# First attention stage: exponentials taken by ScalarE at two shifted arguments and added, in place of tangents and squares, and sequences started one by one

## The reference

```python
    def _L0_xattn_ref(q, k, v):
        scaled = jnp.einsum('bsd,bse->bde', q, k) * scale     # scale = 1/sqrt(256)
        attn = jax.nn.softmax(scaled, axis=1)
        out = jnp.einsum('bde,bse->bsd', attn, v)
        return out
    x = x + _L0_xattn_ref(_layernorm(x, axis=-1), ctx_2048, ctx_2048)
```

## Time and profile before

| what | value |
|---|---|
| median of 3 runs | 1996.21 us (1995.42 to 1996.57) |
| the profiled execution's own time | 2003.36 us |
| its span in the trace | 2001.6 us |
| mean granted TensorE clock | 0.904 of full speed |
| busy: PE, DVE, ACT, POOL | 81%, 69%, 41%, 30% of the span |
| the stage's first VectorE instruction | 12.98 us |
| the stage's last VectorE instruction ends | 79.77 us (79.35 + 0.42) |
| first VectorE instruction of the next stage | 80.58 us |

### The profile page before, as it was taken

The page is one execution under the profiler, slowest core; times in us unless marked ns, Lnnn a source line. Parts: engine busy times, 40 slices in busy tenths (PEclk is TensorE's granted clock), DMA queues, the critical chain, the costliest instruction groups (busy, mean ns, idle before and its releaser), DMA issues. The chain is left out here.

```text
span 2001.6 us, 30042 instructions
## 1 busy us (share of the span) xinstructions
PE 1613.5 (81%) x9326; PEld 1135.7 (57%) x9326; DVE 1387.7 (69%) x3901; ACT 823.7 (41%) x2380; POOL 605.3 (30%) x739
## 2 busy tenths in 40 slices
PE   3559998879353788988889699999987999799883
PEld 2424434356122466666666488788774555688872
DVE  6679969678796688888888634676555333468875
ACT  1113444457332466666667433333331222244451
POOL 0020003067401777777777430111122000321000
PEclk7579999969665999999999899999997999899996
DMA  1305620010382900000000150000035222522200
GB/s 63 110 1 158 194 101 1 13 67 1 9 156 75 343 1 1 2 1 1 1 1 2 31 173 1 26 12 12 11 144 149 75 87 74 179 103 101 69 25 11
DMA packets 103590, 129.34 MB, mean 65 GB/s; under 512 B 14160, under 2 KB 89136, under 8 KB 99984
## 3 DMA queue, kind: packets, MB, share of 16 engines
q1 hardware_dynamic: 94448, 112.39, 17.7%
q0 software_dynamic: 8992, 15.08, 3.6%
...
## 5 line engine op out<-in xcount | busy, mean ns | idle before, releaser
L2326 PE MATMUL l2fa_psQ<-l2fa_xT,l2f_home 128*128 128x128 f32 x1024 | 124.9, 283 | 0.7 <-DMA l2f_home<-in_L2f_kvT 0.7
L2326 PEld LDWEIGHTS l2fa_psQ<-l2fa_xT,l2f_home 128*128 128x128 f32 x1024 | 121.8, 199 | 3.1 <-issue 1.6
L580 POOL TENSOR_TENSOR l0f_diag<-g_identb,l0f_mask 128x1024 bf16<-128x1024 bf16 x16 | 32.0, 2025 | 227.7 <-PE l0f_psA L836 208.8
L2817 ACT ACTIVATE l2x_probs<-l2x_psS,l2x_nmax 128x128 f32<-128x128 f32 x256 | 90.7, 371 | 10.2 <-DVE l2x_nmax L2731 10.0
L2601 POOL TENSOR_TENSOR l2x_probs<-l2x_probs,l2x_rtotal 128x512 f32<-128x512 f32 x64 | 66.8, 1043 | 90.2 <-DVE l2x_rtotal L2737 90.2
L3102 POOL TENSOR_TENSOR route_rrms<-route_vrms,g_minus_half 128x1 f32<-128x1 f32 x8 | 5.7, 707 | 270.6 <-DVE route_vrms L3124 270.6
L2612 POOL TENSOR_TENSOR l2x_vsm<-l2x_vraw,l2x_smooth_row 128x512 f32<-128x512 f32 x64 | 84.7, 1345 | 3.7 <-ACT l2x_vraw L2851 3.4
...
L3511 DVE COPY moe_xgT<-moe_psX 128x256 f32<-128x256 f32 x47 | 20.0, 425 | 91.1 <-PE moe_psX L3617 91.1
L2962 PEld LDWEIGHTS l2x_psS<-l2x_kT,l2x_qT 128*128 128x128 f32 x512 | 66.8, 192 | 22.3 <-issue 17.9
L1427 ACT ACTIVATE l2fa_probs<-l2fa_psS,l2fa_bias 128x128 f32<-128x128 f32 x128 | 45.2, 365 | 76.6 <-DVE l2fa_bias L1411 76.6
L1040 ACT ACTIVATE l1a_probs<-l1a_psS,l1a_nmax 128x256 f32<-128x256 f32 x128 | 58.9, 472 | 42.1 <-PE l1a_psT L1068 29.7
...
## 6 DMA issues: line engine op xcount, KB each, us to landing
...
```

The lines of the kernel that those rows point to most:

```text
L2326: last = nc.tensor.matmul(psQ[bank][:, j, :], w[:, c, h * HD:(h + 1) * HD], xT[u][:, c, :], start=(c == 0), stop=(c == KC - 1))
L2817: last = nc.scalar.activation(probs[:, n % 2, j, :], psS[:, j, :], ACT.Exp, bias=nmax[:, n % 2, j:j + 1], scale=1.0, accum_out=total[:, n ...
```

## The change

The stage is rewritten. ScalarE takes `Exp` straight from the scores, twice: once with the bias of the maximum and once with a bias an eighth larger (`SHIFT`), each with its row sums (two halves each, so four instructions per sequence, L385 of the changed kernel). VectorE adds the two results (L344) and the two sums (L343). The factor 1 + exp(1/8) that both then carry cancels in the division. The tangent, the three steps of `roots` and the squares are gone, and so is the copy of the keys: TensorE reads `G.ctx` itself. The bias takes two instructions where it took one.

Statistics, power and normalisation are now made per sequence: `statistics(b)` is three VectorE instructions (L321 to L323), GpSimd has one power of a single column per sequence (L313), `normalise(b)` one VectorE instruction (L327). `scores(b)` waits for its own sequence, and statistics of later sequences stand between the work on earlier ones. `scores(b + 2)` waits for `probs_ready` of b, since both exponentials read `psS`. The loops are written out in full. Four semaphores go and one comes.

```diff
 def stage_l0_xattn(nc, G, A):
     with ExitStack() as ctx:
         T = Pool(nc, ctx, "l0a")
         q = T.sb("q", [P, B, D])
         alloc_norm(T)
-        k = T.sb("k", [P, 2, D])
         v = T.sb("v", [P, 2, KC, P])
-        probs = T.sb("probs", [P, 2, KC, D])
-        t = T.sb("t", [P, 2, KC, D])
-        den = T.sb("den", [P, KC, D])
+        probs, probs2 = T.sb("probs", [P, 2, KC, D]), T.sb("probs2", [P, 2, KC, D])
         nmax = T.sb("nmax", [P, 2, KC])
-        bias = T.sb("bias", [P, 2, KC])
-        total = T.sb("total", [P, 2, KC])
+        bias = T.sb("bias", [P, 2, 2, KC])
+        total = T.sb("total", [P, 2, 2, KC])
         rtotal = T.sb("rtotal", [P, 2, KC])
...
         scale = D ** -0.5
+        SHIFT = 0.125
 
         with nc.Block() as block:
             @block.gpsimd
             def _(pool):
-                rstd_all(nc, G, T)
+                for b in range(B):
+                    pool.wait_ge(T.var_ready, b + 1)
+                    nc.gpsimd.tensor_tensor(T.rstd[:, b:b + 1], T.ve[:, b:b + 1], G.minus_half[:, 0:1], ALU.pow)\
+                        .then_inc(T.rstd_ready, 1)
 
             @block.vector
             def _(dve):
-                T.order = Order(dve, order)
-                normalise_all(nc, G, T, q)
-                def maxima(b, u):
+                o = Order(dve, order)
+
+                def statistics(b):
+                    o.step(nc.vector.bn_stats(T.stats[:, b, :], G.x[:, b, :]))
+                    o.step(nc.vector.bn_aggr(T.mv[:, b, :], T.stats[:, b, :]))
+                    nc.vector.tensor_scalar(T.ve[:, b:b + 1], T.mv[:, b, 1:2], 1e-5, None, ALU.add).then_inc(T.var_ready, 1)
+
+                def normalise(b):
+                    dve.wait_ge(T.rstd_ready, b + 1)
+                    nc.vector.tensor_scalar(q[:, b, :], G.x[:, b, :], T.mv[:, b, 0:1], T.rstd[:, b:b + 1],
+                                            ALU.subtract, ALU.mult).then_inc(T.ln_ready, 1)
+
+                def maxima(b):
+                    u = b % 2
                     dve.wait_ge(scores_ready, b + 1)
                     nc.vector.tensor_reduce(nmax[:, u, :], psS[u][:, :, :], AX.X, ALU.max, negate=True)\
                         .then_inc(max_taken, 1)
                     dve.wait_ge(max_taken, b + 1)
-                    nc.vector.tensor_scalar(bias[:, u, :], nmax[:, u, :], scale / 4, None, ALU.mult)\
+                    nc.vector.tensor_scalar(bias[:, u, 0, :], nmax[:, u, :], scale, None, ALU.mult)
+                    nc.vector.tensor_scalar(bias[:, u, 1, :], nmax[:, u, :], scale, SHIFT, ALU.mult, ALU.add)\
                         .then_inc(bias_ready, 1)
 
-                def roots(b, u):
-                    dve.wait_ge(tanh_ready, b + 1)
-                    nc.vector.tensor_scalar(den[:, :, :], t[:, u, :, :], -1.0, 1.0, ALU.mult, ALU.add)\
-                        .then_inc(den_ready, 1)
-                    dve.wait_ge(den_ready, 2 * b + 1)
-                    nc.vector.reciprocal(den[:, :, :], den[:, :, :]).then_inc(den_ready, 1)
-                    dve.wait_ge(den_ready, 2 * b + 2)
-                    wait(dve, out_ready, b - 1)
-                    nc.vector.scalar_tensor_tensor(probs[:, u, :, :], t[:, u, :, :], 1.0, den[:, :, :],
-                                                   ALU.add, ALU.mult).then_inc(root_ready, 1)
-                def divide(b, u):
+                def divide(b):
+                    u = b % 2
                     dve.wait_ge(probs_ready, b + 1)
-                    nc.vector.reciprocal(rtotal[:, u, :], total[:, u, :]).then_inc(sum_ready, 1)
-                    dve.wait_ge(sum_ready, b + 1)
+                    nc.vector.tensor_tensor(rtotal[:, u, :], total[:, u, 0, :], total[:, u, 1, :], ALU.add).then_inc(sum_ready, 1)
+                    nc.vector.tensor_tensor(probs[:, u, :, :], probs[:, u, :, :], probs2[:, u, :, :], ALU.add)\
+                        .then_inc(added_up, 1)
+                    dve.wait_ge(sum_ready, 2 * b + 1)
+                    nc.vector.reciprocal(rtotal[:, u, :], rtotal[:, u, :]).then_inc(sum_ready, 1)
+                    dve.wait_ge(sum_ready, 2 * b + 2)
                     wait(dve, out_ready, b - 1)
                     nc.vector.tensor_tensor(v[:, u, :, :], G.ctxT[:, :, b, :],
                                             rtotal[:, u, :].unsqueeze(2).to_broadcast([P, KC, P]), ALU.mult)\
                         .then_inc(v_ready, 1)
 
-                def add(b, u):
+                def add(b):
                     dve.wait_ge(out_ready, b + 1)
-                    nc.vector.tensor_tensor(G.x[:, b, :], G.x[:, b, :], psO[u][:, :], ALU.add)\
-                        .then_inc(added, 1)
-                def step(b, u, next_one):
-                    if next_one:
-                        maxima(b + 1, 1 - u)
-                    divide(b, u)
-                    if next_one:
-                        roots(b + 1, 1 - u)
-                    if not is_zero(b):
-                        add(b - 1, 1 - u)
-                maxima(0, 0)
-                roots(0, 0)
-                one_by_one(dve, step)
-                add(B - 1, 1)
+                    nc.vector.tensor_tensor(G.x[:, b, :], G.x[:, b, :], psO[b % 2][:, :], ALU.add).then_inc(added, 1)
+
+                statistics(0)
+                statistics(1)
+                normalise(0)
+                statistics(2)
+                normalise(1)
+                statistics(3)
+                maxima(0)
+                for b in range(B):
+                    if b + 2 < B:
+                        normalise(b + 2)
+                    if b + 1 < B:
+                        maxima(b + 1)
+                    if b + 4 < B:
+                        statistics(b + 4)
+                    divide(b)
+                    if b > 0:
+                        add(b - 1)
+                add(B - 1)
 
             @block.scalar
             def _(act):
-                def keys(b, u):
-                    wait(act, scores_ready, b - 1)
-                    nc.scalar.copy(k[:, u, :], G.ctx[:, b, :]).then_inc(k_ready, 1)
-                def exponentials(b, u):
+                for b in range(B):
+                    u = b % 2
                     act.wait_ge(bias_ready, b + 1)
-                    wait(act, root_ready, b - 1)
-                    for c in range(KC):
-                        last = nc.scalar.activation(t[:, u, c, :], psS[u][:, c, :], ACT.Tanh,
-                                                    bias=bias[:, u, c:c + 1], scale=scale / 4)
-                    last.then_inc(tanh_ready, 1)
-                    act.wait_ge(root_ready, b + 1)
-                    for c in range(KC):
-                        last = nc.scalar.activation(probs[:, u, c, :], probs[:, u, c, :], ACT.Square,
-                                                    accum_out=total[:, u, c:c + 1])
+                    wait(act, out_ready, b - 1)
+                    for k, e in enumerate((probs, probs2)):
+                        for c in range(KC):
+                            last = nc.scalar.activation(e[:, u, c, :], psS[u][:, c, :], ACT.Exp, bias=bias[:, u, k, c:c + 1],
+                                                        scale=scale, accum_out=total[:, u, k, c:c + 1])
                     last.then_inc(probs_ready, 1)
-                def step(b, u, next_one):
-                    if next_one:
-                        if two_follow(b, next_one):
-                            keys(b + 2, u)
-                        exponentials(b + 1, 1 - u)
-                keys(0, 0)
-                keys(1, 1)
-                exponentials(0, 0)
-                one_by_one(act, step)
 
             @block.tensor
             def _(pe):
-                pe.wait_ge(T.ln_ready, 1)
-                def scores(b, u):
-                    pe.wait_ge(k_ready, b + 1)
-                    wait(pe, tanh_ready, b - 1)
+                def scores(b):
+                    pe.wait_ge(T.ln_ready, b + 1)
+                    wait(pe, probs_ready, b - 1)
                     for c in range(KC):
-                        last = nc.tensor.matmul(psS[u][:, c, :], k[:, u, c * P:(c + 1) * P], q[:, b, :],
+                        last = nc.tensor.matmul(psS[b % 2][:, c, :], G.ctx[:, b, c * P:(c + 1) * P], q[:, b, :],
                                                 start=True, stop=True)
                     last.then_inc(scores_ready, 1)
 
-                def step(b, u, next_one):
-                    if two_follow(b, next_one):
-                        scores(b + 2, u)
+                def values(b):
+                    u = b % 2
+                    pe.wait_ge(added_up, b + 1)
                     pe.wait_ge(v_ready, b + 1)
                     wait(pe, added, b - 1)
                     for c in range(KC):
@@ -424,9 +406,12 @@
                                                 start=(c == 0), stop=(c == KC - 1))
                     last.then_inc(out_ready, 1)
 
-                scores(0, 0)
-                scores(1, 1)
```

(7 more changed lines are left out.)

7 lines of the change are left out of this document (3 added, 4 removed).

## The result

| what | before | after |
|---|---|---|
| median of the runs | 1996.39 us (1995.42 to 1997.03, 4 runs) | 1964.85 us (1963.00 to 1966.20, 4 runs) |
| ratio, with its 95% interval | 1 | 0.9835 (0.9815 to 0.9855) |
| profiled execution, its span, clock | 2003.36 us, 2001.6 us, 0.904 | 1963.00 us, 1961.3 us, 0.916 |
| last addition of the stage ends | 79.77 us | 44.40 us |
| next stage starts | 80.58 us | 45.20 us |

The change saves 31.5 us in the median. In the profiled executions the stage is 35.4 us shorter (79.77 - 44.40), and the spans differ by 40.3.

What follows compares the result with a forecast made beforehand. VectorE's list, over half of it one reciprocal, was taken as the bound. Stage end 45.4 plus 1.2 for GpSimd's power gave 46.6 us, 33.2 less than 79.77; 1996.21 - 33.2 = 1963.0 us, range 1959.5 to 1967.0.

Steps and rivals of the forecast that it cites:

- The bound: In the stage's loop, VectorE's list sets the 6.58 us per sequence, over half of it one reciprocal of 3.35 us.
- The start: Before the loop, sequence 0 alone is prepared, so first scores start at 15.4 us, 5.7 us earlier.
- The periods: VectorE's list per sequence takes 3.65 us with statistics and 2.9 without; the last division starts at 42.4 us.
- GpSimd's power beside VectorE: In the loop and at the start, GpSimd's powers hold VectorE up on shared ports: 1.2 us, between 0 and 2.6.
- The clock: TensorE's granted clock rises from 0.50 by some 30 us, so a matmul block takes 0.93 us and VectorE is the bound.
- rival 1: In the stage, the clock stays at 0.50 and blocks of 1.86 us set the pace; end 49.2, total 1965.6 us; chance 0.24.
- The stage's end: Last addition to x: 45.4 us plus 1.2 for GpSimd's power gives 46.6, 33.2 us less than before.
- Its sign of being wrong: Wrong if the stage ends before 44 or after 50 us, or the next stages' lengths change by over 2 us.
- From the stage to the total: Behind the barrier, the stage's 33.2 us come off the whole in full: median 1996.21 to 1963.0 us.
- Serial sequences (2): In the loop, sequences don't overlap, 9.2 us each; stage ends at 89.0, total 2005.4 us; chance 0.02.
- Next stage warm (3): TensorE arrives warm in the next stage, saving up to 5 us of its first matmuls; total 1958 us; chance 0.05.
- No change (4): The change fails its claim or later stages wait the gain away; total stays 1996 us; chance 0.01.

Runs made afterwards that it cites:

- experiment 8: Changed kernel without the second exponential, its bias and both sums, output off by 0.021; 1960.78 us in one execution, stage end 37.33.
- Experiment 5: Changed kernel with the sum of the two exponentials' tiles on GpSimd in place of VectorE; 1967.43 us in one execution, stage end 46.32.
- Experiment 9: Changed kernel with two extra matmuls into an unread tile behind each product from sequence 3 to 6; 1964.36 us in one execution, stage end 43.63.
- experiment 1: The changed kernel again, unaltered; 1962.44 us (6 runs), ratio 0.981 to the kernel before, stage end 43.97.
- experiment 4: Changed kernel with one unused reciprocal (3.35 us) on VectorE behind the last addition to x; 1969.95 us, ratio 0.9839.
- experiments 3 and 7: 3: one-by-one start alone against the kernel before, 1992.43 us; 7: TensorE adding the exponentials, against the changed kernel, 1970.70 us, and the changed kernel again, 1960.54 us.

## Why the prediction was right, and where not

The forecast was 1963.0 us; the first measurement gave 1964.85, the later two of the changed kernel 1962.44 and 1960.54. The mechanism was right; that the total came within 2 us was in part luck, as the last step shows. By its steps:

- **The bound.** Right. VectorE's list with the reciprocal set the 6.58 us, and without it the period fell to 3.47 and 2.72. That VectorE is still the bound is shown by experiment 8 (0.73 us out of its list gave 0.73 per period) and by the windows.
- **The start.** First scores forecast at 15.4, came at 15.00. I took 1.0 for the first power, as if the 1.005 of the earlier trace rows were its first use; it took 0.56. That was a wrong reading, answered under GpSimd's power below.
- **The periods.** Forecast 3.3, 3.65, 3.65, 2.9, 2.9, 2.6, 2.1; read 3.13, 3.47, 3.47, 2.72, 2.73, 2.40, 2.16. Most were about 0.2 too long: I had 0.10 for a small instruction start to start, and it is 0.07. The last division was forecast to start at 42.4 and started at 40.50.
- **GpSimd's power beside VectorE.** The term of 1.2 us was wrong; it cost VectorE nothing that the rows show. The sum L344 is 0.69 with the power beside it and without, and the power grew from 0.56 to 1.00. The trace before already held this. The 1.005 us of the earlier trace rows is the fifth of the eight powers, and it started 0.17 us behind an instruction of VectorE:

```profile
1406.22 0.58 DVE L1584 TENSOR_SCALAR l2fa_gw<-l2fa_gw,l2fa_winv 128x704 f32<-128x704 f32 x1
1406.39 1.00 POOL L3102 TENSOR_TENSOR route_rrms<-route_vrms,g_minus_half 128x1 f32<-128x1 f32 x1 [34.70 <-DVE route_vrms L3124]
```

The term came from a row in which VectorE's instruction came second; here VectorE comes first and GpSimd pays, with time it has. Experiment 5 shows the other order: VectorE's normalisation grew from 0.41 to 1.36 behind GpSimd's sum. The Trainium skill's page SBUF — State Buffer, section "SBUF: two separate sides", gives the pair of ports that the two engines share to whichever of them starts first. The sum L344 and the normalisations of experiment 5 agree with it. So the 2.6 us that the prediction drew from this page was a misreading: it left out who starts first. The page's rule didn't show everywhere: in experiment 8 a power started at 22.82 and the two-source product L345 at 22.85, and both kept their times (0.55 and 0.43). In the changed kernel itself the values L350 started at 27.89, inside a power (27.19 to 28.19), and kept their 0.42.
- **The clock.** Right that it rises (1.00 from about 26 us), so rival 1 fell. Wrong at the end: it fell again at 39.7, and the last product took 2.05 and not 1.1. From the start of the last division to the end I had 3.0 us, and it was 3.9. Experiment 9 bought 0.7 to 0.95 of it back by keeping TensorE at work. TensorE's short pauses were named in rival 1 as a reason for such a fall, and left out of the forecast.
- **The stage's end.** 46.6 forecast, 44.40 read. The difference of 2.2 is 1.9 in the start and the periods, and 1.2 for the power, less 0.9 for the clock. Most of the prediction's own marks were thus missed on the fast side: first scores before 15.4, sums 3.13 to 3.47 apart in place of 3.6 to 4.2, the last addition before 45. Its sign of being wrong, an end before 44, was not met at 44.40 but was at 43.97 in experiment 1. The other, a change of over 2 us in later stages, was met too (1482.1 to 1478.9 for the rest), but two executions of one kernel differ by more, so that sign could not tell anything.
- **From the stage to the total.** This was the weak step: "I take the same difference off". The barrier does pass the stage's gain on: it moved the next stage's start by 35.38 us, and experiment 4's 3.3 likewise. But the median fell by 31.5 us in the first measurement, by 38.0 and 36.6 in the next two, and the stage's 35.4 lies between these. The forecast of the total lay within 2 us of the first median because a stage forecast 2.2 us too long met a measurement that showed 3.8 us less gain than the stage: two errors of opposite sign, which is luck. The text reckoned that 0.2% (4 us) could be told from no change; single executions of one kernel differ by up to 17 us on one chip, and medians of 4 to 12 runs of the kernel before by 4. In experiments 3 and 7 the total is off by 4 and 11 us from what the stage gives, beyond the intervals.
- **Rivals.** Serial sequences (2): no, periods of 2.7 to 3.5 and not 9. Next stage warm (3): no, its TensorE work began at 0.50 as before, and the first feed-forward's length, 315.7, lies within the 314.7 to 318.7 of all kernels here. Its 5 us were worked out from no row. No change (4): no; but its thought that later stages' phases of the clock move was nearer than the chance of 0.01 says, as a scatter in both directions and not as a loss.

Of the versions tried none is shown to beat the changed kernel in total time. TensorE adding the exponentials shortens the stage by about 1 us, while its total was 11.5 us lower in one execution and 10.2 us higher in four; why is open.
